# A state-space convolution, an LSTM-like recurrence and a head on one core: GpSimd makes the weights' quarter differences, TensorE transposes the first unit, each tile's two parts go in one DMA transpose, and units and loads come in another order

## The chip, the cores and the metric

The kernel runs on one core of a Trainium2 chip. Its engines work side by side and are tied by semaphores: TensorE (PE: matmuls, and PEld: its weight loads), VectorE (DVE), ScalarE (ACT), GpSimd (POOL) and SyncE (SP), which here issues every DMA; its row is SPq. The metric is the device time in microseconds (us) from the kernel's start to its end, lower is better. The kernel before took 2893.31 us (median of 3 runs, 2892.33 to 2895.29).

## The reference, cut to what matters

```python
x = L0_attn_r                                   # (8, 2048, 512) float32
# 1. state-space layer: K from (B, C, P, Q, Lam, step), a causal convolution over the 2048 rows
h1 = irfft(rfft(norm(x), n=4096) * rfft(K, n=4096))[:, :2048]
x = x + layernorm(gelu(h1 + D * norm(x)))
# 2. a recurrence over the first axis b = 0..7, with 2048 rows x 512 channels as batch
for xt in x:
    ft = sigmoid(xt @ wf.T + c @ uf.T + bf)
    it = sigmoid(xt @ wi.T + c @ ui.T + bi)
    gt = tanh(xt @ wc.T + c @ uc.T + bc)
    c  = ft * c + it * gt                       # c starts as in_c in every row
h = tanh(x @ wo.T + c_final @ uo.T + bo)
x = x + layernorm(h)
```

## The kernel before

**Stages.** From 0 to about 140 us x's statistics and the convolution kernel are made. From there to 640 us the convolution runs in 16 iterations (`i` = 1 to 16), one for each group of 32 channels, each of 16 places `j`. From 640 to 2503 us the recurrence runs, and from there to the end the head (the matmul with wo, tanh, norm, store), 128 tiles of 128 rows.

**Convolution.** In place `j` of iteration `i` PE advances the state of group i (L1700, L1708), applies a power of the state matrix (L1724) and convolves two channels of group i-1 (L1738, L1746). ACT and DVE copy every state and every product of powers out of PSUM as a float16 high part (ACT L923, L934) and a low part (DVE L1276, L1286), and PE's next step waits for them. GpSimd meanwhile normalizes the 4 pieces of group i+1, two operations of 128x1024 a piece (L806 subtracts, L808 multiplies). Beside this the weights are prepared: `weight_places()` puts each step of each of 16 weight loads at an `(i, j)`. Load n is matrix wf, uf, wi, ui, wc, uc, wo or uo; for n % 4 < 2 its largest value is sought (`most`), otherwise it is cut. The six gate matrices are cut into seven "quarters" of 256x256 (a scheme with 7 products for a 2 by 2 block matmul): W11, W21, W22, W12 of the matrix, and three of the four differences made by the step `sum`, which DVE does at L1379, 128x512 each, 4 for each matrix, in iterations 2, 3, 6, 7, 10 and 11 at places 7 to 10. ACT makes each quarter's high part (`hi`, L1009), DVE its low part (`lo`, L1395). `start` is DVE's sum of uf, ui or uc weighted with in_c (L1384, L1386), which stands in for `c @ u.T` where b = 0; it is stored in accd.

**Recurrence.** A unit is 512 rows of one b: b from 0 to 7, and j from 0 to 3 for which quarter of the 2048 rows. There are 32 units, in the order of `unit(u)`: first j = 0 and 1 in turn over all b, then j = 2 and 3. So units 0, 1, 16 and 17 have b = 0 and no product with the state: 42 matmuls a gate group in place of 84. Each unit has 6 gate groups (192 in all); at group n PE makes the products, ACT copies (L1109, L1118, L1125) and applies sigmoid or tanh (L1095), DVE adds (L1557, L1565) and updates the state. Before its products a unit must be prepared in six stages, `prepare(stage, v)` on every engine: load the convolution's result from yd (`load_y`) and x (`load_x1`); DVE's statistics (L1411, L1412), GpSimd's `rate`, ACT's norm (L1017), DVE's `add` of x with statistics (L1419 to L1421), a store of the sum (`store_x1`), a second norm, DVE's `row_sums` (L1436 to L1439, after the store has landed, since they overwrite the tile), the cut in a high part (ACT L1036) and a low part (DVE L1448), and SP's `turn`, which transposes the two parts of each of 8 tiles with a DMA transpose each (L588), 16 a unit. `PREP_AT` says at which gate group each stage of each unit stands: unit 1 at groups 0 to 5, unit 2 at 6 to 11, unit 3 at 12 to 17; units 4, 5 and 6 have only 5 groups each, and from unit 7 on a unit's stages start 9 groups ahead of its own first group. Unit 0's six stages come between convolution and recurrence. Each engine works through its own list in order, and SP's list is one DMA queue, so that order of issue is order of service.

## Time and profile before

| | us |
|---|---|
| median of 3 runs | 2893.31 |
| the profiled execution's own time | 2893.05 |
| its span | 2891.3 |
| PE busy | 2603.2 (90%) |
| PE weight loads | 2105.0 (73%) |
| DVE busy | 1944.9 (67%) |
| ACT busy | 1504.9 (52%) |
| POOL busy | 901.2 (31%) |
| granted TensorE clock, mean | 0.956 of full speed |

"Busy" is time in which the engine executes; an engine that waits is idle. PE is the longest, so what the kernel can lose is mostly time in which PE waits, or runs at the lower clock after it has waited. The rows below come from this one execution.

### The profile page before, as it was taken

Reading aid. Unit: us, or ns where it says so; the run is one execution under the profiler, and the core shown is the slowest. Engines: PE = TensorE matmul, PEld = TensorE weight load, DVE = VectorE, ACT = ScalarE, POOL = GpSimd, SP = SyncE. Lnnn points to the kernel's source line nnn. Section 1 sums busy time; section 2 is a strip of 40 time slices with the busy share of each in tenths; the row PEclk is TensorE's granted clock in tenths of the full one; section 3 lists DMA queues with packets and bytes.
Section 4 is the critical chain, followed back from the end, with each engine's and each line's share of the span. In section 5 each row is a group of like instructions: output and inputs, shape, how many; then the busy total and the mean of one; then the engine's idle time right before and its main releaser. Section 6 shows DMA issues by size and latency. Waiting matters only on the chain.

```text
span 2891.3 us, 55063 instructions
## 1 busy us (share of the span) xinstructions
PE 2603.2 (90%) x21475; PEld 2105.0 (73%) x21475; DVE 1944.9 (67%) x3424; ACT 1504.9 (52%) x2802; POOL 901.2 (31%) x1425
## 2 busy tenths in 40 slices
PE   4598998983679889999999779999999999999997
PEld 4377777873467778888888668888888888744443
DVE  7766667553656666777667577667677775477777
ACT  6655555553544554555555465555455554344444
POOL 7766565521112211211221221221121120043333
PEclk9699999996899999999999989999999999999999
DMA  9877776786444445444534544545644554187776
GB/s 330 289 231 256 244 266 233 266 308 207 112 116 113 99 107 124 121 99 117 130 99 108 155 124 119 128 100 102 124 122 100 121 128 110 62 300 267 268 264 236
DMA packets 541188, 492.06 MB, mean 170 GB/s; under 512 B 292224, under 2 KB 423552, under 8 KB 535680
## 3 DMA queue, kind: packets, MB, share of 16 engines
q1 hardware_dynamic: 540928, 488.56, 57.7%
q8 instruction: 168, 2.75, 0.4%
q14 instruction: 92, 0.75, 0.1%
HBM read 270.60 MB, written 150.73 MB: 146 GB/s over the span
## 4 chain that ended last, share of the span: by engine, by line
PE 53%; DVE 13%; SPq 10%; DMA 9%; ACT 8%; issue 5%; POOL 2%; DVEq 0%; POOLq 0%; ACTq 0%
PE bank L1834 16%; PE bank L1844 15%; SPq L588 9%; PE bank L1902 9%; DMA big<-yd 6%; PE bank L1738 3%; PE bank L1688 3%; ACT big L1095 2%; PE bank L1746 2%; PE bank L1724 2%; DVE big L1539 2%; PE bank L1886 1%; DVE big L1542 1%; DVE big L1379 1%; PE bank L1700 1%
## 5 line engine op out<-in xcount | busy, mean ns | idle before, releaser
L1834 PE MATMUL bank<-big 128*128 128x256 f16 x8064 | 1103.4, 277 | 154.2 <-DMA big<-big 46.7
L1834 PEld LDWEIGHTS bank<-big 128*128 128x128 f16 x8064 | 796.9, 99 | 273.2 <-ACT big L1109 44.1
L1844 PE MATMUL bank<-big 128*128 128x256 f16 x7056 | 967.6, 274 | 0.0
L1844 PEld LDWEIGHTS bank<-big 128*128 128x128 f16 x7056 | 692.9, 98 | 82.2
L851 POOL TENSOR_SCALAR big<-big 128x1 f32<-128x1 f32 x256 | 57.1, 223 | 1397.8 <-DVE big L1412 961.9
L1017 ACT ACTIVATE big<-big 128x512 f32<-128x512 f32 x256 | 206.5, 808 | 272.6 <-POOL big L853 272.1
L1902 PE MATMUL bank<-big 128*128 128x512 f16 x1536 | 332.2, 379 | 0.0
L1095 ACT ACTIVATE big<-big 128x512 f32<-128x512 f32 x384 | 290.9, 805 | 42.4 <-DVE big L1565 42.0
L1902 PEld LDWEIGHTS bank<-big 128*128 128x128 f16 x1536 | 150.3, 98 | 181.2
L1565 DVE TENSOR_TENSOR big<-bank,big 128x512 f32<-128x512 f32 x192 | 130.5, 680 | 182.5 <-PE bank L1844 171.5
L1125 ACT ACTIVATE big<-bank 128x512 f32<-128x512 f32 x192 | 113.3, 590 | 201.0 <-PE bank L1844 191.2
L1411 DVE BATCH_NORM_STATS2 big<-big 128x6 f32<-128x512 f32 x128 | 88.6, 692 | 190.5 <-DMA big<-yd 188.2
L852 POOL TENSOR_TENSOR big<-big 128x1 f32<-128x1 f32 x256 | 200.7, 784 | 21.4
L1118 ACT ACTIVATE big<-bank 128x256 f32<-128x256 f32 x192 | 72.2, 376 | 258.0 <-PE bank L1844 184.6
L806 POOL TENSOR_TENSOR big<-big 128x1024 f32<-128x1024 f32 x63 | 154.6, 2454 | 166.3 <-DMA big<-xg 166.2
L1286 DVE SCALAR_TENSOR_TENSOR big<-bank,big 128x320 f16<-128x320 f32 (+6 forms) x237 | 108.6, 458 | 143.5 <-ACT big L934 143.2
L1135 ACT ACTIVATE big<-big 128x512 f32<-128x512 f32 x128 | 80.7, 630 | 203.8 <-DVE big L1579 203.8
L1448 DVE TENSOR_TENSOR big<-big 128x512 f16<-128x512 f32 x256 | 165.6, 685 | 30.3 <-ACT big L1036 30.1
L1557 DVE TENSOR_TENSOR big<-bank,big 128x512 f32<-128x512 f32 x192 | 131.7, 686 | 76.4 <-ACT big L1109 76.4
L1036 ACT ACTIVATE big<-big 128x512 f16<-128x512 f32 x256 | 153.4, 620 | 48.4 <-DMA big<-big 22.8
L1688 PE MATMUL bank<-big 128*128 128x256 f32 x480 | 152.0, 400 | 15.1 <-DVE big L1268 9.4
L1738 PE MATMUL bank<-big 128*128 128x128 f32 x1024 | 160.8, 280 | 2.1 <-POOL big L817 2.1
(202 smaller groups left out, 3611.5 us busy)
## 6 DMA issues: line engine op xcount, KB each, us to landing
big<-xr SPq DMA_DIRECT2D x16, 2048.0 KB, 10.8
big<-xg SPq DMA_DIRECT2D x64, 512.0 KB, 6.5
big<-kpad SPq DMA_DIRECT2D x32, 1024.0 KB, 12.1
yd<-big SPq DMA_DIRECT2D x16, 2048.0 KB, 17.2
big<-x SPq DMA_DIRECT2D x128, 256.0 KB, 3.1
x1d<-big SPq DMA_DIRECT2D x128, 256.0 KB, 2.0
xtd<-big SPq DMA_DIRECT2D x64, 512.0 KB, 4.6
big<-xtd SPq DMA_DIRECT2D x64, 512.0 KB, 3.9
```

Of the source, the lines that this page charges most:

```text
L588: e.dma_start_transpose(slot[v % 2][:, k, l, :, 128 * p:128 * p + 128], xs16[k][:, l, :]).then_inc(s[f"xq{k}"], 16)
L806: e.tensor_tensor(ug, ug, st(0), SUB).then_inc(s["sub"], 1)
L852: rp().tensor_tensor(st[:, 7:8], st[:, 7:8], mhalf, ALU.pow).then_inc(s["rp"], 1)
L1017: return e.activation(yt[:, :, c, :], e_in, ACT.Identity, bias=st[:, 6:7], scale=st[:, 7:8])
L1036: e.activation(xs16[k][:, 0, :].rearrange("p (g h) -> p g h", g=NG), source(i), ACT.Copy).then_inc(s["xh"], 1)
L1095: e.activation(zt[g][:, r::2, :], zt[g][:, r::2, :], ACT.Tanh if g == 2 else ACT.Sigmoid, bias=bs[:, g, a + 2 * r:a + 2 * r + 1], scale=in ...
L1448: e.tensor_tensor(lo, source(i), hi, SUB).then_inc(s["xlo"], 1)
L1688: ins = e.matmul(o, Gm, u[g % 3][:, k].rearrange("p h b -> p (h b)"), start=True, stop=(k == 0))
L1738: e.matmul(o, T[t % 3][:, h % 16, :], u[g % 3][:, :, h, :], start=(q == 0), stop=False, skip_group_check=True)
L1834: ins = e.matmul(o, WX[2 * g + lw][:, q, kt, 128 * a:128 * a + 128], slot[u % 2][:, part, lx, k0 + kt, :], start=(first and kt == 0 and (l ...
L1844: ins = e.matmul(o, WC[2 * g + lw][:, q, kt, 128 * a:128 * a + 128], cc[u % 2][:, qc, lx, kt, :], start=False, stop=end, skip_group_check= ...
L1902: ins = e.matmul(bank[n % NB_][:, :], xt4[r % NXR][:, lx, kt, 128 * c:128 * c + 128], Wo[:, lw, kt, :], start=(a == 0), stop=(a == 11))
```

## The change

- **Differences.** DVE's step `sum` is gone; GpSimd makes the four differences of a matrix in one go (`quarter_sums`), between the norm of one piece and the next: after the second piece of its iteration, in iteration 2 after the third. The `hi` steps start at place 8 (9 in iteration 2), the `lo` steps one place after each, at 9 to 15 (iteration 2: 10 to 15 and the first of iteration 3).
- **`start` of uf** is done from load 1, at places 0 to 3 of iteration 2, and no longer from load 3; loads 2 and 3 are issued later for it.
- **Unit 0** is no longer prepared in six stages. DVE takes the statistics of the first 15 groups of channels before the last group is done; the second norm writes to other tiles (x0, xs0), so that nothing waits for the store of x1; PE transposes the 8 tiles in float32 into PSUM, and ACT and DVE take the high and low parts from there into the matmuls' operand.
- **SP's order** around this: the load of accd, the last weight stores and loads, and unit 1's loads of x and y ahead of the loads of the state weights (WC).
- **Transposes.** `turn` issues one DMA transpose of 128x1024 for both parts, 8 a unit instead of 16.
- **Order of units**: (7,0), (0,2), (7,1), (0,3) stand at 14 to 17, so that the units with b = 0 of the second half stand at 15 and 17. `last_unit(u)` replaces u - 2 in the waits.
- **`PREP_AT`**: units 1 to 4 take 5 groups each, 1 to 5, 6 to 10, 11 to 15, 16 to 20; then 6 each, 9 groups ahead.
- **Head**: DVE's last addition of a tile comes one tile later (`h - 3` for `h - 2`).

```diff
@@ weight_places
         elif n == 1:
+            places += [("start", f, 2, f) for f in range(4)]
         else:
-            at[n, -1].append(("load", n, 0))
+            at[n, {2: 3, 3: 0}.get(n, -1)].append(("load", n, 0))
...
-                places = [("sum", r, n, 7 + r) for r in range(4)]
-                places += [("hi", q, n, 7 + q) for q in range(7)]
-                places += [("lo", q, n, (9, 11, 12, 13, 14, 15, 15)[q]) for q in range(7)]
+                first = 9 if n == 2 else 8
+                places = [("hi", q, n, min(first + q + (q > 2 and n > 2), 15)) for q in range(7)]
+                places += [("lo", q, n + (first + 1 + q) // 16, (first + 1 + q) % 16) for q in range(7)]
@@ units
+ORDER = [(b, j) for b in range(7) for j in (0, 1)] + [(7, 0), (0, 2), (7, 1), (0, 3)] + [(b, j) for b in range(1, 8) for j in (2, 3)]
 def unit(u):
-    return u % 16 // 2, 2 * (u // 16) + u % 2
+    return ORDER[u]
@@ prep_schedule
-        if v <= 3:
-            places = [6 * (v - 1) + r for r in range(6)]
-        elif v <= 6:
-            first = 18 + 5 * (v - 4)
-            places = [first, first + 1, first + 2, first + 3, first + 4, first + 4]
+        if v <= 4:
+            places = ((1, 2, 3, 4, 5, 5), (6, 7, 8, 9, 10, 10), (11, 12, 13, 14, 15, 15), (16, 17, 18, 19, 20, 20))[v - 1]
@@ SP: turn
-                for l in range(2):
-                    e.dma_start_transpose(slot[v % 2][:, k, l, :, 128 * p:128 * p + 128], xs16[k][:, l, :]).then_inc(s[f"xq{k}"], 16)
+                e.dma_start_transpose(slot[v % 2][:, k].rearrange("p l k t -> p (l k) t")[:, :, 128 * p:128 * p + 128],
+                                      xs16[k].rearrange("p l h -> p (l h)")).then_inc(s[f"xq{k}"], 16)
@@ SP, between convolution and recurrence
+            w.wait_ge(s["accs"], 16 * 3)
+            e.dma_start(fbs, accd.rearrange("g p h -> p g h")).then_inc(s["accs"], 16)
             load_WX(4)
             load_WX(5)
...
+            store_y(NG - 2)
             store_y(NG - 1)
+            w.wait_ge(s["cv"], G * NG)
+            for r in range(4):
+                store_x1(0, r)
+            for c in CHUNKS:
+                load_x1(1, c)
+            load_y(1)
...
+            for n in range(6):
+                load_WC(n)
+            store_xt(0)
@@ GpSimd
+            def quarter_sums(n):
+                m = 2 * (n // 4) + n % 2
+                w.wait_ge(s["w"], 16 * (n + 1))
+                w.wait_ge(s["w_hi"], low_base(m))
+                w.wait_ge(s["w_lo"], low_base(m))
+                for o, p0, p1 in ((Wt[0], W12, W11), (Wt[1], W22, Wt[0]), (W12, W22, W12), (Wt[2], W21, Wt[1])):
+                    ws().tensor_tensor(o, p0, p1, SUB).then_inc(s["w_sum"], 1)
+            for i in range(1, NG - 1):
+                for q in range(4):
+                    norm(4 * (i + 1) + q)
+                    if i < 12 and i % 4 >= 2 and q == (2 if i == 2 else 1):
+                        quarter_sums(i)
@@ PE, ahead of unit 0 (ACT's high and DVE's low read bank[2 + i % 6])
+            for i in range(8):
...
+                for kt in range(4):
+                    ins = e.transpose(bank[2 + i % 6][:, kt * 128:(kt + 1) * 128], source(i)[:, kt * 128:(kt + 1) * 128], ident)
@@ DVE, ahead of unit 0
+            for n in range(4):
+                stat(n)
+            w.wait_ge(s["fb"], 12)
+            e.tensor_tensor(bias0, bank[0][:, 0:12].rearrange("p (g m) -> p g m", g=3), bias, ADD).then_inc(s["yc"], 1)
+            for n in range(4):
+                add(n)
+            row_sums(0, 0)
+            low(0)
+            row_sums(0, 1)
+            for i in range(1, 8):
+                low(i)
```

The order on VectorE in iteration 6, places 7 to 11, before (L1379 is `sum`, L1395 `lo`, L1276 and L1286 the parts that PE's next step waits for):

```order
362 L1379 TENSOR_TENSOR big<-big 128x512
363 L1276 SCALAR_TENSOR_TENSOR big<-bank,big 128x256
364 L1286 SCALAR_TENSOR_TENSOR big<-bank,big 128x8x32
365 L1379 TENSOR_TENSOR big<-big 128x512
366 L1276 SCALAR_TENSOR_TENSOR big<-bank,big 128x256
367 L1286 SCALAR_TENSOR_TENSOR big<-bank,big 128x6x64
368 L1379 TENSOR_TENSOR big<-big 128x2x256
369 L1395 SCALAR_TENSOR_TENSOR big<-big 128x512
```

and after, from place 9 on (L1432 is `lo`, L1323 and L1333 are L1276 and L1286):

```order
360 L1432 SCALAR_TENSOR_TENSOR big<-big 128x512
361 L1323 SCALAR_TENSOR_TENSOR big<-bank,big 128x256
362 L1333 SCALAR_TENSOR_TENSOR big<-bank,big 128x6x64
363 L1432 SCALAR_TENSOR_TENSOR big<-big 128x512
364 L1323 SCALAR_TENSOR_TENSOR big<-bank,big 128x256
365 L1333 SCALAR_TENSOR_TENSOR big<-bank,big 128x5x64
366 L1432 SCALAR_TENSOR_TENSOR big<-big 128x512
```

The four differences are gone from DVE's list, and the low parts stand one at a place from 9 on. On GpSimd the four stand in iteration 6 after the second of four pieces (L824 and L826 are L806 and L808, L869 the differences):

```order
184 L824 TENSOR_TENSOR big<-big 128x1024
185 L826 TENSOR_TENSOR big<-big 128x1024
186 L824 TENSOR_TENSOR big<-big 128x1024
187 L826 TENSOR_TENSOR big<-big 128x1024
188 L869 TENSOR_TENSOR big<-big 128x512 x2
189 L869 TENSOR_TENSOR big<-big 128x2x256
190 L869 TENSOR_TENSOR big<-big 128x512
191 L824 TENSOR_TENSOR big<-big 128x1024
192 L826 TENSOR_TENSOR big<-big 128x1024
```

The norm of the third and fourth piece now comes behind them. SP's list from the end of the convolution to unit 1's first transposes, before:

```order
114 L557 DMA big<-yd 128x14x128
115 L572 DMA big<-x 128x512 x4
116 L470 DMA yd<-big 128x4096
117 L475 DMA big<-wg 128x3584 x2
118 L630 DMA big<-accd 128x3x512
119 L480 DMA big<-wg 128x3584 x3
120 L470 DMA yd<-big 128x4096
121 L480 DMA big<-wg 128x3584 x3
122 L577 DMA x1d<-big 128x512 x4
123 L588 DMA_TRANSPOSE big<-big 128x4x128 x12
124 L572 DMA big<-x 128x512 x2
125 L564 DMA big<-yd 128x16x128
```

and after:

```order
114 L568 DMA big<-yd 128x14x128
115 L587 DMA big<-x 128x512 x4
116 L643 DMA big<-accd 128x3x512
117 L486 DMA big<-wg 128x3584 x2
118 L481 DMA yd<-big 128x4096 x2
119 L592 DMA x1d<-big 128x512 x4
120 L587 DMA big<-x 128x512 x4
121 L576 DMA big<-yd 128x16x128
122 L491 DMA big<-wg 128x3584 x6
123 L609 DMA xtd<-big 128x2048 x2
124 L592 DMA x1d<-big 128x512 x4
125 L602 DMA_TRANSPOSE big<-big 128x8x128 x6
```

The load of accd moved ahead of two weight loads and a store, unit 0's transposes are gone, and unit 1's x and y stand ahead of the six state weight loads.

## Rows read from the trace of the kernel before

**Rows 1.** Iterations 3, 5, 6, 7; length; busy of PE, PEld, DVE, ACT, POOL; clock; DMA
```profile
204.80:246.90 42.10, 33.85 (x282) 27.62 (x279) 30.77 (x47) 20.81 (x45) 20.63 (x8) 0.88 0.65 225
276.80:306.50 29.70, 29.61 (x285) 25.11 (x282) 17.18 (x41) 16.66 (x38) 19.05 (x8) 1.00 0.73 248
306.50:342.60 36.10, 30.98 (x280) 25.73 (x278) 24.55 (x44) 20.70 (x45) 20.11 (x8) 0.95 0.63 212
342.60:378.80 36.20, 29.96 (x282) 24.66 (x279) 27.14 (x43) 20.59 (x45) 20.56 (x8) 1.00 0.74 255
```

**Rows 2.** Waits of PE from 190 to 640 us: for whom, us, times, longest
```profile
PE bank L1708 <- DVE big L1276: 33.9, 27, 4.1
```

**Rows 3.** Groups by line, 190 to 640 us: busy us, mean ns, idle before
```profile
L1379 DVE TENSOR_TENSOR big<-big 128x512 f32<-128x512 f32 x24 | 44.0, 1834 | 0.0
L1395 DVE SCALAR_TENSOR_TENSOR big<-big 128x512 f16<-128x512 f32 x42 | 40.8, 995 | 0.0
```

**Rows 4.** Timeline of iteration 6, DVE and POOL: start, us, engine, line
```profile
329.52 2.70 POOL L808 TENSOR_TENSOR big<-big 128x1024 f32<-128x1024 f32 x1
329.91 2.86 DVE L1395 SCALAR_TENSOR_TENSOR big<-big 128x512 f16<-128x512 f32 x1
333.49 0.67 DVE L1379 TENSOR_TENSOR big<-big 128x512 f32<-128x512 f32 x1
```

**Rows 5.** Timeline of PE from the convolution's end: start, us, [idle before <-releaser]
```profile
652.99 5.25 PE L1820 MATMUL bank<-big 128*128 128x1 f32 x24 [12.68 <-DMA big<-accd]
690.00 1.44 PE L1834 MATMUL bank<-big 128*128 128x256 f16 x6 [31.76 <-issue]
700.86 4.45 PE L1834 MATMUL bank<-big 128*128 128x256 f16 x20 [9.42 <-DMA big<-big]
```

**Rows 6.** Timeline of SP's queue, 640 to 700 us
```profile
648.41 27.05 SPq L577 DMA_DIRECT2D x1d<-big  x4
675.56 15.75 SPq L588 DMA_TRANSPOSE big<-big  x12
...
692.53 0.38 SPq L564 DMA_DIRECT2D big<-yd  x1
```

**Rows 7.** Line 630, the load of accd issued at 637.4 us: issue to landing
```profile
DMA to landing us min/median/max: 15.4/15.4/15.4
```

**Rows 8.** Timeline of DVE, preparation of unit 0, and unit 1's first statistics
```profile
645.21 0.69 DVE L1419 TENSOR_TENSOR big<-big 128x512 f32<-128x512 f32 x1
...
646.98 0.69 DVE L1419 TENSOR_TENSOR big<-big 128x512 f32<-128x512 f32 x1
...
672.70 0.42 DVE L1436 TENSOR_TENSOR big<-big 128x256 f32<-128x256 f32 x1 [12.39 <-DMA x1d<-big]
...
699.84 0.69 DVE L1411 BATCH_NORM_STATS2 big<-big 128x6 f32<-128x512 f32 x1 [11.19 <-DMA big<-yd]
```

**Rows 9.** Stretches: unit 0, unit 1, units 2 to 5, unit 6, unit 16
```profile
700.90:747.70 46.80, 30.88 (x247) 25.11 (x248) 28.59 (x54) 24.77 (x44) 10.71 (x25) 0.83 0.54 135
747.70:805.20 57.50, 35.71 (x258) 27.42 (x258) 38.43 (x67) 29.73 (x52) 10.67 (x25) 0.80 0.44 110
805.20:1064.70 259.50, 231.41 (x2020) 201.67 (x2021) 166.50 (x276) 126.32 (x217) 56.31 (x117) 0.94 0.43 108
1064.70:1120.00 55.30, 54.36 (x499) 48.48 (x498) 38.66 (x63) 30.01 (x52) 11.49 (x24) 1.00 0.49 115
1622.50:1676.50 54.00, 36.40 (x292) 30.04 (x290) 36.30 (x64) 31.25 (x55) 10.92 (x25) 0.84 0.53 140
```

**Rows 10.** Waits of PE from 805 to 1065 us
```profile
PE bank L1834 <- ACT big L1109: 13.4, 4, 7.2
```

**Rows 11.** Line 588, the transposes, 1060 to 1560 us: ns min/median/max, and landing
```profile
L588 SPq DMA_TRANSPOSE big<-big x144: 1188/1266/5400, 1070.9 to 1543.3; - x144
...
DMA to landing us min/median/max: 2.4/2.5/8.5
```

**Rows 12.** The chain that ended last, in the head: start, us, what
```profile
2700.40 82.88 PE bank L1902 x384
```

More of the change, by code:

```diff
@@ L311, in s4_lstm_program @@
         junk = take(1)
+        st0 = [take(12) for _ in range(4)]
         winv = win.rearrange("p (k o) -> p k o", k=4)
@@ L841, in pool_program @@
             norm(7)
-            for n in range(8, 4 * NG):
-                norm(n)
+            ws = Chain(w, s, "w_sum")
+            def quarter_sums(n):
[10 more added lines that the diff above has]
+                        quarter_sums(i)
             rp = Chain(w, s, "rp")
@@ L866, in prepare @@
                     rate(4 * v + 3, "2")
-            for stage in range(1, 7):
-                prepare(stage, 0)
+            for n in range(4):
+                rate(n, "1")
+            for n in range(4):
+                rate(n, "2")
             for n in range(GROUPS):
@@ L1069, in state_high @@
             def state_high(u, place):
-                c16, last = cc[u % 2], unit(u)[0] == 7
+                b, j = unit(u)
+                c16, c32, last = cc[j % 2], cf[j % 2], b == 7
                 if place == 0:
@@ L1491, in state_sums @@
             def state_sums(u, place):
-                c32, last = cf[u % 2], unit(u)[0] == 7
+                c32, last = cf[unit(u)[1] % 2], unit(u)[0] == 7
                 base = state_parts(u - 1) if u else 0
```

171 lines of the change are left out of this document (99 added, 72 removed).

## The prediction

> **What bounds the kernel now.** I read the page's busy shares and slices first: PE is busy 90% of the span, so what can be saved is where PE waits or runs at the lower clock. The busy times by stretch show three such places. In the convolution most iterations last 29.7 us with PE busy in nearly all of it, while iterations 6 and 7, with the same number of matmuls, last 36.1 and 36.2 us, and iteration 3 lasts 42.1 [rows 1]. Iterations 10 and 11 look like 6 and 7 (35.6 and 36.9 us between the same points). PE's waits there are on DVE's low part of the state, 33.9 us in 27 waits [rows 2]. The second place is 640 to 701 us, where PE does almost nothing [rows 5]. The third is the recurrence's units that PE does not fill: a settled unit lasts 55.3 us with PE busy 54.4, but unit 0, with half the matmuls, lasts 46.8, unit 1 57.5 and unit 16 54.0, and units 2 to 5 last 259.5 where four settled ones would be 221 [rows 9]. In the head the chain of waits is PE without a gap [rows 12]. Everything else is PE at 2.4 GHz and isn't touched.
>
> **The convolution.** The edit takes 24 differences, 44.0 us in all, off DVE [rows 3]. Their time alone isn't the cost. One such difference takes 0.67 us when GpSimd is idle; a low part that starts 0.39 us after a GpSimd multiply takes 2.86 us, ending 0.55 after it [rows 4]. So the two engines exclude one another when both read SBUF with two operands, and DVE loses up to 2.1 us beyond its 0.74. Of 42 low parts only the excess of (0.995 - 0.74) x 42 = 10.7 us is there, five or six long ones: the low parts of an iteration now come mostly after GpSimd has ended its norm. That cover goes. GpSimd has 8 operations of 2.4 us (busy 19 to 20 us of an iteration) [rows 1], and four differences of half the elements, 1.2 us each, come between them: 25 of 29.7 us. It will then be busy at places 9 to 15, where the low parts now stand. By places (1.8 us each), GpSimd starting about 5 us into iteration 6 as now (its last multiply ends at 332.2 [rows 4], 25.7 in, of which 20.1 busy): two pieces to 15, differences to 20, two pieces to 30. The low parts at places 9, 10, 11 (16 to 20 us) meet short operations, those at 12 and 13 (21 to 25) long ones; those at 14 and 15 have no close follower, since no state is advanced at 15. A long meeting makes a place 2.9 us instead of 1.8, so 1.1 each; a short one I take at 0.2. That is 2.8 us, near 3 with the clock, against 36.1 - 29.7 = 6.4 today. Iterations 6, 7, 10, 11: 4 x 3.7 = 15. Iteration 3 has `start` and the differences today, 42.1 - 29.7 = 12.4; left with 4, it gives 8. Iteration 2 gets `start` at places 0 to 3 and later loads: it loses 1. Sum -22. Bounds: the excess of all six iterations is 45 (no meeting costs anything); if each of five low parts an iteration costs the full 2.1, 6 x 10.5 = 63 is left instead of 45: 18 slower.
>
> The Trainium skill ("SBUF — State Buffer", section "SBUF: two separate sides") says that VectorE and GpSimd share a port pair as an exclusive lock held for the whole instruction, for a VectorE operation with two SBUF inputs among others. It speaks against the edit: the lock time isn't removed but moved to the other side of it. The 2.86 us agree. By the rule alone, with the low parts always met, the second bound would be nearer.
>
> **Convolution to recurrence.** Today: convolution ends at 640.3, the load of accd lands 15.4 us after its issue [rows 7], the bias matmuls run 653.0 to 658.2 [rows 5], unit 0's row sums wait 12.4 us for the store of x1 [rows 8], which lies behind six weight loads and two stores, then the transposes take 675.6 to 691.3 with a row of their own each [rows 6], and PE's products run steadily from 700.9 [rows 5]. After: accd lies only behind y and x, so about 645.5 by the same queue; bias matmuls 5.2, to 650.7. DVE now waits for them before its four `add`s, 1.77 us each [rows 8], to 657.9. Row sums 1.8 (659.7), rate, second norm and first high part (660.7), its low part, row sums of the other half 663.2, PE's transposes of the last two tiles about 3 (at the rate of the 24 small float32 matmuls in 5.25 us [rows 5], 1.8 for a tile's four), their high and low parts 1.3: PE starts near 669. That is 32 us. Nothing else is late: the weights of the inputs land before, the state weights (six loads of 0.9 MB) are first needed by unit 2, 100 us later.
>
> Unit 1's y can be issued when six tiles are cut, 667, and lands 7.3 later, 674.5 (today 692.5 to 699.8 [rows 6, 8]). Its preparation took 699.8 to 747.7, 48 us, by the chain DVE, GpSimd, ACT, SP, not by PE [rows 9]; I take 47 in five groups. Unit 1 starts at 721.5 instead of 747.7: -26 up to here. Its own length stays 57.5: PE's 12 short groups of units 0 and 1 are fewer than preparation needs. Unit 2 starts with its transposes already landed, but in unit 1's last group DVE waits for unit 3's y.
>
> Units 2 to 5 hold 38 us beyond four settled ones [rows 9]. Partly these are waits for transposes and partly the wait for y, 11.2 us for DVE in the first case [rows 8], which reaches PE through ACT L1109 (13.4 us, up to 7.2) [rows 10] and costs clock on top. It is exposed where stages 5 and 6 of one unit and stage 1 of the next stand in adjacent groups, today at three places in units 3 to 5, and the transposes come last at two more. After, two such places are left (groups 16 and 21), about 10 us each: 38 becomes 21, -17. Sum of this part: -43. Bounds: if the 5-group schedule costs as much as today, -26; if the excess vanishes and units 0 and 1 follow at PE's pace, -75.
>
> **One transpose for two.** A transpose now takes 1.27 us of SP's queue, in a chain of 2.5 to landing [rows 11]; 16 are 20 us of a 55 us unit. The larger one isn't in the trace: between 1.27 us (a cost per instruction) and twice or more. Twelve took 15.75, 1.31 each, with hardly a gap [rows 6], and each moves 128 KB; I take the double, 2.5, so nothing gained. The Trainium skill ("DMA: Bandwidth & Descriptors", section "Why a DMA increments its semaphore by 16 and not by 1") gives for the sequencers before the newest chip a push command per tile of a transpose, so a cost in proportion to size; the sum would be the same.
>
> **Order of units.** Unit 16 is 26 us longer than PE's half unit; 10 of it is DVE's wait for y. That wait stays, in units 15 and 17 now, since stage 1 still falls in the middle of every unit. What a long unit between them gives is one group of slack once more: -3, between +5 and -15. **Head**: PE is the bound without gaps [rows 12], so DVE's later addition is worth 0; if it made DVE late, the last tile's addition of about 0.7 us is all that the end could see.
>
> **The sum.** -22 - 43 - 3 = -68 on the profiled execution's 2893.05 (span 2891.3; median of the runs 2893.31, the same within 0.3): 2825 us.
>
> **Rivals.**
> A. *The lock eats the convolution's gain.* All exposed low parts meet long operations: no gain or a loss of up to 18 there. For it: GpSimd is made busier exactly where low parts stand. Against it: the differences are short, and five places an iteration are exposed, not seven. With 0 there: 2847.
> B. *The merged transpose costs as one.* For it: it is one instruction, and the queue's 1.27 us hardly vary; against it, the size. SP's 12 transposes ahead of the y load shrink by 8 us; where y and the last transposes are exposed (units 0 to 3, 15, 17), 3 to 4 us each: -20. 2805.
> C. *The recurrence starts no earlier than its data*: stores of y and x1, unit 1's x and y and the state weights share one queue, and unit 1's x1 store lands behind 5.4 MB of weights. Today's wait of that kind was 12.4 us [rows 8]. With 15 us lost: 2840.
> D. *Slower: the merged transpose is worse than two.* Place: SP's queue. A unit there has 8 merged transposes and about 6 us of other issues; PE's unit is 55. From about 6 us each the queue is as long as the unit. Each further us costs 8 us in 28 long units, 224; the gain of 68 is gone at 6.3 us, and at 7 us the time is about 3050. Nothing in the trace shows such a cost, only that the shape is new.
>
> **Chances.** Forecast 0.45 (2800 to 2850), A 0.2, B 0.18, C 0.12, D 0.05. The range 2790 to 2862 holds the forecast, A, B and C, each with some 15 us of its own uncertainty cut off at the edge. A measurement of this kernel can tell 0.2%, 6 us, from no change: faster 0.94, same 0.01, slower 0.05.
>
> **What would show it.** In iterations 6, 7, 10, 11: length near 33 us, no differences on DVE, low parts of 1.3 to 2.9 us at places 12 and 13. At 2.86 everywhere, or lengths over 36, A holds. PE's products start near 669 less what the convolution gave (about 647 on the new clock of events), unit 1 some 52 us later. The transposes' row: 2.5 us is the forecast, 1.3 is B, over 6 is D. Units 2 to 5 near 242 us. Units 15 and 17 with PE idle some 18 us each; if it is under 8, slack was worth more than I gave it. The forecast is wrong if the recurrence's settled units differ from 55.3 us, which nothing here should touch.

## The result, and the profile after

The kernel after took 2778.23 us (median of 4 runs, 2775.45 to 2780.31), the kernel before 2893.85 on the same chip (4 runs, 2892.33 to 2895.29): ratio 0.96, 95% interval 0.9583 to 0.9617. It is 115.6 us faster; 68 were forecast, and 2778 lies below the range. The profiled executions differ by as much: span 2891.3 before, and from the page of the kernel after (its first line, and PE's busy time):

```profile
span 2777.9 us, 54870 instructions
...
PE 2591.0 (93%) x21507; PEld 2101.9 (76%) x21507; DVE 1941.2 (70%) x3404; ACT 1511.5 (54%) x2802; POOL 959.8 (35%) x1449
```

Cut at the same instructions in both traces, the 113.4 us of the spans lie here (us; "forecast" is the prediction's own term for the stretch; the convolution is taken from PE's first to its last matmul of L1738, L1799 after, "steady products" begin at 700.9 before and 644.9 after):

| stretch | before | after | change | forecast |
|---|---|---|---|---|
| to the convolution's first matmul | 138.7 | 137.5 | -1.2 | 0 |
| convolution, 16 iterations | 501.1 | 481.8 | -19.3 | -22 |
| its end to the steady products | 61.1 | 25.7 | -35.4 | -32 |
| recurrence (to the head's first matmul with wo) | 1812.9 | 1760.8 | -52.1 | -14 |
| head | 377.5 | 372.1 | -5.4 | 0 |

**Convolution.** Stretches of the kernel after, iterations 3, 6, 7 (length, busy of PE, PEld, DVE, ACT, POOL, clock, DMA), against [rows 1]:

```profile
204.60:237.30 32.70, 29.55 (x280) 24.68 (x278) 21.27 (x37) 20.44 (x46) 23.17 (x11) 1.00 0.84 294
...
298.20:329.70 31.50, 29.45 (x281) 24.76 (x280) 21.01 (x38) 19.71 (x44) 25.58 (x12) 1.00 0.74 256
329.70:362.30 32.60, 29.95 (x280) 24.81 (x278) 22.24 (x38) 20.54 (x46) 23.02 (x12) 1.00 0.81 282
```

Iterations 6, 7, 10 and 11 together went from 144.9 to 128.8, iteration 3 from 42.1 to 32.7, iteration 2 from 34.1 to 35.2. But 4, 8 and 12, which were 29.9, 29.3 and 29.3, are 31.3, 31.1 and 31.1. These are single executions: in the profiles of the experiments below that leave the convolution as it is, it takes 497.6 to 501.0 us in the kernel before and 481.1 to 484.8 in the kernel after (iteration 3 alone 39.5 to 41.8 and 32.7 to 37.0), so the gain is known to some 4 us. GpSimd is busy 25.6 of 31.5 us in iteration 6, and DVE's low parts meet it. Groups by line, 190 to 620 us of the kernel after, for [rows 3]:

```profile
L1432 DVE SCALAR_TENSOR_TENSOR big<-big 128x512 f16<-128x512 f32 x42 | 65.4, 1568 | 0.0
...
L869 POOL TENSOR_TENSOR big<-big 128x512 f32<-128x512 f32 x24 | 32.6, 1357 | 3.3 <-DMA big<-wts 1.9
```

A low part now takes 1.57 us in the mean instead of 0.995. The timeline of DVE's low parts in iteration 6:

```profile
318.12 0.96 DVE L1432 SCALAR_TENSOR_TENSOR big<-big 128x512 f16<-128x512 f32 x1
...
320.04 1.85 DVE L1432 SCALAR_TENSOR_TENSOR big<-big 128x512 f16<-128x512 f32 x1
...
322.54 2.13 DVE L1432 SCALAR_TENSOR_TENSOR big<-big 128x512 f16<-128x512 f32 x1
...
325.33 2.14 DVE L1432 SCALAR_TENSOR_TENSOR big<-big 128x512 f16<-128x512 f32 x1
...
330.93 0.73 DVE L1432 SCALAR_TENSOR_TENSOR big<-big 128x512 f16<-128x512 f32 x1
```

and of GpSimd there, the differences and the norm of the pieces behind them:

```profile
313.22 5.31 POOL L869 TENSOR_TENSOR big<-big 128x512 f32<-128x512 f32 x4
318.49 2.85 POOL L824 TENSOR_TENSOR big<-big 128x1024 f32<-128x1024 f32 x1
321.42 2.71 POOL L826 TENSOR_TENSOR big<-big 128x1024 f32<-128x1024 f32 x1
324.08 2.83 POOL L824 TENSOR_TENSOR big<-big 128x1024 f32<-128x1024 f32 x1
326.99 2.72 POOL L826 TENSOR_TENSOR big<-big 128x1024 f32<-128x1024 f32 x1
```

While GpSimd works on 128x1024, each low part waits and ends 0.55 us after the GpSimd operation that it met (at 321.34, 324.13 and 326.91), which by then has been followed by the next; the one at 330.93, past GpSimd's last multiply (329.7), takes 0.73. Each of these meetings costs the low part 1.1 to 1.4 us. The full 2.0 to 2.1 us of [rows 4] is still there once in each of iterations 3, 7 and 11, where a low part of 2.78 us starts just behind a GpSimd operation. In each of iterations 6, 7, 10 and 11 four low parts last 1.85 us or more. PE's waits on DVE's low part of the state, 190 to 620 us, for [rows 2]:

```profile
PE bank L1769 <- DVE big L1323: 18.4, 21, 1.7
```

33.9 us became 18.4, and the longest wait 1.7 instead of 4.1.

**Convolution to recurrence.** Timeline of PE in the kernel after, for [rows 5] (start, us, and in brackets the idle time before it and its releaser):

```profile
623.27 4.72 PE L1881 MATMUL bank<-big 128*128 128x1 f32 x24 [3.45 <-DMA big<-accd]
632.29 1.11 PE L1892 MATMUL bank<-big 128*128 128x128 f32 x4 [4.30 <-ACT big L1050]
...
641.41 0.63 PE L1892 MATMUL bank<-big 128*128 128x128 f32 x4 [0.50 <-DVE big L1498]
644.95 2.29 PE L1909 MATMUL bank<-big 128*128 128x256 f16 x10 [2.91 <-issue]
```

The wait for accd is 3.45 us instead of 12.68, PE's own transposes (L1892) take 632.3 to 642.0, and products run from 644.95.

**Recurrence.** Stretches of the kernel after: unit 0, unit 1, units 2 to 5, unit 6, for [rows 9]:

```profile
644.70:693.60 48.90, 31.55 (x252) 24.62 (x252) 29.53 (x55) 25.06 (x44) 9.38 (x24) 0.88 0.80 250
693.60:747.00 53.40, 36.82 (x261) 28.16 (x262) 37.82 (x67) 27.83 (x49) 11.00 (x26) 0.82 0.51 123
747.00:982.00 235.00, 224.74 (x1998) 197.89 (x1997) 165.85 (x274) 127.61 (x218) 54.55 (x116) 0.97 0.49 118
982.00:1037.00 55.00, 55.00 (x506) 49.29 (x505) 39.53 (x64) 30.35 (x52) 11.75 (x24) 1.00 0.48 116
```

Units 2 to 5 take 235.0 (259.5 before), and a settled unit has PE busy in all of its 55.00 us. The transposes, 980 to 1430 us, for [rows 11]:

```profile
L602 SPq DMA_TRANSPOSE big<-big x64: 1232/1290/3390, 990.5 to 1396.9; - x64
...
DMA to landing us min/median/max: 3.1/3.4/6.6
```

One transpose of 128x1024 takes 1.29 us of the queue, where one of 128x512 took 1.27. It costs as one, not as two. What that does is seen in SP's queue. One settled unit of the kernel before, from the stores of x1 (L577) over 12 transposes (L588) and two loads of x (L572) to the load of the next unit's y (L564):

```profile
1108.40 18.45 SPq L577 DMA_DIRECT2D x1d<-big  x4
1127.02 18.11 SPq L588 DMA_TRANSPOSE big<-big  x12
1145.17 1.06 SPq L572 DMA_DIRECT2D big<-x  x2
1146.27 0.43 SPq L564 DMA_DIRECT2D big<-yd  x1
```

and of the kernel after (L592, L602, L587, L576):

```profile
1024.23 21.09 SPq L592 DMA_DIRECT2D x1d<-big  x4
1045.49 13.31 SPq L602 DMA_TRANSPOSE big<-big  x6
1058.86 1.05 SPq L587 DMA_DIRECT2D big<-x  x2
1062.03 0.38 SPq L576 DMA_DIRECT2D big<-yd  x1
```

Before, the y load follows the x loads without a gap, 19.2 us after the first transpose, and in the last 12 us before it the queue is never idle: the queue sets when it goes. After, it goes 16.5 us after it, and 2.1 us of that SP waits for DVE's row sums, which free y's tile: now the data set it. DVE's waits for y in the whole execution of the kernel before (us in total, times, longest):

```profile
DVE big L1411 <- DMA big<-yd: 188.2, 31, 11.2
```

and of the kernel after:

```profile
DVE big L1455 <- DMA big<-yd: 79.9, 30, 8.6
```

How such a wait reaches PE, in a settled unit of the kernel before: DVE's first statistics of the next unit,

```profile
1153.98 0.69 DVE L1411 BATCH_NORM_STATS2 big<-big 128x6 f32<-128x512 f32 x1 [5.39 <-DMA big<-yd]
```

and PE 9 us on:

```profile
1162.90 0.83 PE L1834 MATMUL bank<-big 128*128 128x256 f16 x6 [1.04 <-ACT big L1118]
```

DVE stands still for 5.39 us with the gates' additions behind it. ACT's sigmoid (L1095) waits for such an addition, DVE's next additions for the sigmoid, ACT's copy (L1118) for these, and PE for the copy: it loses 1.04. From 980 to 1100 us of the kernel after DVE's wait is 1.5 to 1.7 us, and PE has none.

### The profile page after: what moved, and what is told of

Read it like the earlier page. It is cut to its first block, busy times and chain, and to the rows that moved or that the text cites. A ratio compares the mean times of both kernels' runs of the same rounds, so it can differ in the third digit from the quotient of the medians.

```text
span 2777.9 us, 54870 instructions
## 1 busy us (share of the span) xinstructions
PE 2591.0 (93%) x21507; PEld 2101.9 (76%) x21507; DVE 1941.2 (70%) x3404; ACT 1511.5 (54%) x2802; POOL 959.8 (35%) x1449
## 4 chain that ended last, share of the span: by engine, by line
PE 80%; DVE 8%; DMA 4%; ACT 3%; issue 2%; POOL 1%; SPq 1%; DVEq 0%; POOLq 0%; ACTq 0%
PE bank L1909 28%; PE bank L1919 27%; PE bank L1977 12%; PE bank L1749 3%; PE bank L1799 3%; PE bank L1785 2%; PE bank L1807 2%; DVE big L1432 2%; PE bank L1961 1%; DMA big<-yd 1%; PE bank L1761 1%; DMA big<-big 1%; DMA big<-xr 1%; DVE big L1344 1%; PE bank L1769 1%
## 5 line engine op out<-in xcount | busy, mean ns | idle before, releaser
L1333 DVE SCALAR_TENSOR_TENSOR big<-bank,big 128x320 f16<-128x320 f32 (+6 forms) x237 | 108.5, 458 | 140.4 <-ACT big L968 140.1
L824 POOL TENSOR_TENSOR big<-big 128x1024 f32<-128x1024 f32 x63 | 154.1, 2446 | 111.6 <-DMA big<-xg 111.4
L1504 DVE TENSOR_TENSOR big<-big 128x512 f16<-128x512 f32 x248 | 159.8, 684 | 6.7 <-ACT big L1077 6.6
L1799 PE MATMUL bank<-big 128*128 128x128 f32 x1024 | 159.1, 278 | 2.1 <-POOL big L835 2.1
L826 POOL TENSOR_TENSOR big<-big 128x1024 f32<-128x1024 f32 x63 | 154.8, 2457 | 4.9
## 6 DMA issues: line engine op xcount, KB each, us to landing
big<-xr SPq DMA_DIRECT2D x16, 2048.0 KB, 11.1
```

The lines of the kernel that those rows point to most:

```text
L824: e.tensor_tensor(ug, ug, st(0), SUB).then_inc(s["sub"], 1)
L826: e.tensor_tensor(ug, ug, st(1), MUL).then_inc(s["nrm"], 1)
L1504: e.tensor_tensor(lo, source(i), hi, SUB).then_inc(s["xlo"], 1)
L1799: e.matmul(o, T[t % 3][:, h % 16, :], u[g % 3][:, :, h, :], start=(q == 0), stop=False, skip_group_check=True)
```

## The experiments

The kernel before took 2893.9 to 2900.7 us on the chips used; differences under some 6 us between kernels of different chips are therefore read from stretches of the profile, not from medians. "Marks" of units are ACT's copies (L1109 before, L1156 after), one a gate group; the first six units lie between the first mark and the 37th. Stretches scatter too: five other profiles of the kernel after whose edits lie outside the first six units (experiments 6 and 8 to 10) or change the transposes' number alone (13) have 336 to 337 us there, where the kernel after's own has 340.7.

**1. The merged transpose alone** (kernel before, with it).

```diff
-                for l in range(2):
-                    e.dma_start_transpose(slot[v % 2][:, k, l, :, 128 * p:128 * p + 128], xs16[k][:, l, :])...
+                e.dma_start_transpose(slot[v % 2][:, k].rearrange("p l k t -> p (l k) t")[:, :, 128 * p:128 * p + 128], xs16[k].rearrange("p l h -> p (l h)"))...
...
```

> The kernel before with one DMA transpose for both parts of a tile, nothing else changed. Theory 1 (the larger transpose costs SP's queue as much as one small one, 1.29 us, so that the y load comes earlier in every unit and the small stalls of the settled units go): 25 to 45 us faster than before, the settled units at 55.0 us each as in the changed kernel. Theory 2 (the forecast's: cost in proportion to size, the shorter settled units come from another part of the change): within 5 us of before, and settled units of 55.2 to 56 us.

2818.51 us (2816.33 to 2819.36), before on that chip 2897.17: ratio 0.9734 [0.972, 0.9749], 79 us faster by one edit that was priced at nothing, and far more than theory 1's 25 to 45. DVE's waits for y:

```profile
DVE big L1411 <- DMA big<-yd: 82.8, 31, 8.0
```

**2. All but the merged transpose** (kernel after, with two again: edit 1 backwards).

> The changed kernel with two DMA transposes a tile again. Theory 1: it gives back 25 to 45 us, to 2803 to 2823. Theory 2: within 5 us of 2778. If it gives back clearly less than the same edit brings to the kernel before, the other parts of the change have hidden part of the cost.

2837.54 us (2832.77 to 2841.55): ratio 0.98 [0.9782, 0.9818], 58 us slower than experiment 6 (the kernel after with the old order of units) on the same chip; again more than the 25 to 45 expected. All other parts together bring 56 to 60, where the sum had 68. The same edit brings the kernel before 79, so the other parts hide some 20 of it. DVE's waits for y are back:

```profile
DVE big L1455 <- DMA big<-yd: 177.9, 30, 9.7
```

**3. The y load earlier, two transposes** (kernel of experiment 2, in SP's list of a unit).

```diff
                 if stage == 5:
-                    for k in range(2, 6):
-                        turn(8 * v + k)
-                    if v + 1 < NU:
-                        load_x1(v + 1, 0)
-                        load_x1(v + 1, 2)
+                    turn(8 * v + 2)
+                    turn(8 * v + 3)
                 if stage == 6:
                     if v + 1 < NU:
                         load_y(v + 1)
+                    turn(8 * v + 4)
+                    turn(8 * v + 5)
+                    if v + 1 < NU:
+                        load_x1(v + 1, 0)
+                        load_x1(v + 1, 2)
```

> The kernel after with two transposes a tile again (2837.5 us by itself, 59 more than with one), and with the y load ahead of the transposes of tiles 4 and 5 and of the loads of x. Theory (two transposes cost 59 us because some 5 us more of queue stand ahead of the y load in each unit): with four transposes fewer ahead of it a good part of the 59 comes back, 2785 to 2810, and the waits for y, 177.9 us in 30 waits without the move, fall below 110. Rival (what two transposes cost is their own landing and the products that wait for tiles): it stays at 2830 or more.

2776.36 us (2773.12 to 2777.1): ratio 0.9576 [0.9556, 0.9596]. All 61 us are back, more than the theory gave, though its 16 transposes a unit fill the queue as before. DVE's waits for y are 52.5 us. The queue in a settled unit, with 8 transposes ahead of y in place of 12:

```profile
1043.59 12.75 SPq L603 DMA_TRANSPOSE big<-big  x8
1060.11 0.38 SPq L576 DMA_DIRECT2D big<-yd  x1
```

It goes 16.5 us after the first transpose, as in the kernel after. So the 61 us come back by a shorter queue ahead of the y load, with the transposes' own number and landing as they were. That the merged transpose gains nothing by its own landing doesn't follow: see experiment 5.

**4. The same in the kernel before** (that edit alone).

> The kernel before with one edit: the load of the next unit's y ahead of the transposes of tiles 4 and 5 and of the two loads of x in SP's list of a unit; still two transposes a tile. Theory (what the merged transpose brought is queue time ahead of the y load, and any edit that lets this load start earlier brings the same): as in the kernel before with merged transposes, 2800 to 2830, and the waits for y, 188 us in 31 waits, fall below 100. Rival (in the kernel before something else holds the units, the early load brings only what the kernel after leaves on it, 14 us): 2870 to 2885.

2837.91 us (2834.48 to 2841.91): ratio 0.9792 [0.977, 0.9813], 62 us faster, 8 outside the theory's interval and far from the rival's. The waits for y fall to 55.3 us. Merging brings 17 to 19 us more than this in the kernel before, though the early y load leaves DVE less to wait: 10.0 of them by the recurrence's first mark (3.4 of these in the convolution, which neither edit touches, the others where unit 0 is transposed), 11.7 in units 0 to 5. The sum of the waits is thus a sign and not a price.

**5. The y load earlier in the kernel after** (edit of experiment 3).

> The kernel after, with the load of the next unit's y put into SP's list of a unit ahead of the transposes of tiles 4 and 5 and of the two loads of x, instead of behind them. Theory (what the merged transpose gave back is time that stood ahead of the y load in that queue, and the rest of the wait for y, 79.9 us in 30 waits in the kernel after, is more of the same): the waits for y fall by half or more, the time falls by 20 to 40 us, to 2740 to 2760. Rival (the wait for y in the kernel after is set by when the exchange of y is written, not by the queue; the merged transpose gained by its own landing): within 5 us of the kernel after, 2773 to 2783; if tiles 4 and 5 then come late to the products, up to 10 us slower.

2764.56 us (2763.65 to 2772.0): ratio 0.954 [0.9519, 0.9561]. 14 us faster than the kernel after: between theory and rival. The waits fall only to

```profile
DVE big L1457 <- DMA big<-yd: 59.1, 30, 3.3
```

because SP now waits for the row sums: 56.1 us in 8 units of 980 to 1430 us (22.9 in the kernel after):

```profile
SPq L576 <- DVE big L1493: 56.1, 8, 7.1
```

The gain lies in units 0 to 5 (327.9 us by marks, 340.7 after) and 15 and 17; settled units have nothing left to give. Against experiment 3, which differs from this one in the merging alone and ran on the same chip (2776.36), it is 11.8 us faster, 11.0 of them in units 0 to 5: there the merged transpose still brings something when y is early. Whether that is the transposes' landing or the rest of the queue was not tried apart.

The recurrence of seven kernels, us between marks:

| kernel | units 0-5 | 6-17 | 18-30 | DVE's waits for y |
|---|---|---|---|---|
| before | 364.8 | 656.9 | 727.1 | 188.2 |
| before, merged (1) | 330.1 | 641.3 | 715.3 | 82.8 |
| before, y early (4) | 341.8 | 639.2 | 715.3 | 55.3 |
| after, split (2) | 363.2 | 660.1 | 726.4 | 177.9 |
| after, split, y early (3) | 338.9 | 636.1 | 715.8 | 52.5 |
| after | 340.7 | 641.3 | 715.3 | 79.9 |
| after, y early (5) | 327.9 | 635.8 | 715.3 | 59.1 |

715.3 is 13 units of 55.0, PE's own time. Every kernel here that gets y early, by either edit, reaches it within 0.5; with the rest of the change alone it is 726.4.

**6. The old order of units** (kernel after).

```diff
-ORDER = [(b, j) for b in range(7) for j in (0, 1)] + [(7, 0), (0, 2), (7, 1), (0, 3)] + [(b, j) for b in range(1, 8) for j in (2, 3)]
+ORDER = [(b, j) for b in range(8) for j in (0, 1)] + [(b, j) for b in range(8) for j in (2, 3)]
```

> The changed kernel with the old order of units (all of j = 0 and 1, then j = 2 and 3), so that both short units of the second half stand next to each other at 16 and 17; the preparation's schedule as in the changed kernel. Theory 1 (each short unit pays DVE's wait for y and the preparation's chain by itself, wherever it stands): 0 to 4 us slower than the changed kernel. Theory 2 (a long unit between the short ones gives back slack, and that is the 10 us found in units 14 to 17 beyond the 3 forecast): 7 to 12 us slower.

2779.22 us (2777.11 to 2781.08): ratio 0.9599 [0.9585, 0.9614]. No difference. Units 14 to 17 take 201.2 us by marks, with the new order 201.1.

**7. The old places of preparation** (kernel after, `PREP_AT` of units 1 to 6 as before).

> The changed kernel with the old places of units 1 to 6 in the preparation's schedule (unit 1 at groups 0 to 5, 6 groups each up to unit 3, 5 groups each for units 4 to 6). Theory 1 (as in the forecast: the new places take one exposed wait for y and the late transposes of units 2 to 4 away): 12 to 20 us slower than the changed kernel. Rival (with the cheaper transpose and the earlier y the places hardly matter): under 5 us slower.

2773.86 us (2772.61 to 2780.37): ratio 0.9568 [0.9551, 0.9584]. If anything faster: from the first products to the head's first matmul 1753.2 us against 1760.8, and against 1756.4 to 1757.3 in experiments 6, 8, 9, 10 and 13. Once the merged transpose is there, the five-group places bring nothing. What they bring with two transposes was not tried.

**8. The differences on DVE** (kernel after; `sum`, the places of `hi` and `lo`, `start` and the loads as before).

```diff
+                places = [("sum", r, n, 7 + r) for r in range(4)]
+                places += [("hi", q, n, 7 + q) for q in range(7)]
+                places += [("lo", q, n, (9, 11, 12, 13, 14, 15, 15)[q]) for q in range(7)]
...
-                    if i < 12 and i % 4 >= 2 and q == (2 if i == 2 else 1):
-                        quarter_sums(i)
```

> The changed kernel with the quarter differences back on DVE, at the old places, and loads and start steps as before. Theory 1 (as in the forecast): it gives back what the convolution brought, 19 us between the same points of the two traces, so 17 to 21 us slower than the changed kernel, iterations 6 and 7 at 36 us. Rival (the convolution's shorter time comes from other loads and is not the differences): under 8 us.

2794.09 us (2791.8 to 2796.81): ratio 0.9633 [0.9619, 0.9648], 16 slower than the kernel after. Theory 1 holds, a little short of its 17 to 21. The convolution takes 499.0 us against 481.8, iterations 3, 6, 7, 10, 11: 39.6, 34.6, 36.8, 36.7, 37.3.

**9. GpSimd nearly idle where low parts stand** (kernel after; in iterations 6, 7, 10 and 11 the norm of pieces 3 and 4 is done on 8 elements a row instead of 1024, so most of it is left out).

```diff
...
+                if g in (7, 8, 11, 12) and q >= 2:
+                    ug, st0_, st1_ = ug[:, 0:1, 0:1], st0_[:, 0:1, 0:1], st1_[:, 0:1, 0:1]
...
```

> The changed kernel in which GpSimd leaves out most of the norm of the third and fourth piece of the input in iterations 6, 7, 10 and 11 (the two operations act on 8 elements a row instead of 1024), so that GpSimd is idle while DVE makes its low parts. Theory 1 (DVE's low parts wait for GpSimd's operations, which exclude them from SBUF): low parts of 0.74 us there, iterations 6, 7, 10, 11 at 29.5 to 30 instead of 31.5 to 32.7 us, 7 to 11 us faster in all. Rival (they last longer because of ACT's high parts or of DVE's own list): no change within 2 us.

2763.29 us (2762.31 to 2764.65): ratio 0.9527 [0.9513, 0.9541], and 14.5 less than experiment 13 (2777.81, no different from the kernel after) on the same chip, where 7 to 11 were expected. Its iterations 6 and 7:

```profile
300.90:330.00 29.10, 29.03 (x281) 24.69 (x279) 17.14 (x40) 19.67 (x44) 15.75 (x12) 1.00 0.82 280
330.00:359.90 29.90, 29.38 (x281) 24.76 (x279) 18.00 (x38) 20.37 (x46) 16.44 (x12) 1.00 0.88 309
```

All four are PE's own 29.1 to 29.9 us (10.5 less together, as expected), and so are 8 and 12 (29.6, where the kernel after has 31.1; another 3.0): the excess there was GpSimd's work that had slid into them. With GpSimd quiet the low parts take 0.73 to 0.75 us each and cost PE nothing. PE's waits, 190 to 620 us:

```profile
PE bank L1772 <- DVE big L1326: 6.8, 9, 1.7
```

**10. The norm in halves** (kernel after; pieces 3 and 4 in iterations 2, 3, 6, 7, 10, 11, each operation as two of 128x512).

```diff
+                cuts = ((0, 2), (2, 4)) if g in (3, 4, 7, 8, 11, 12) and q >= 2 else ((0, 4),)
...
+                    for a, b_ in cuts:
+                        ins = e.tensor_tensor(ug[:, a:b_], ug[:, a:b_], st(r)[:, a:b_], op)
```

> The kernel after with GpSimd's normalisation of pieces 3 and 4 in iterations 2, 3, 6, 7, 10 and 11 in operations of half the size (128x512 elements instead of 128x1024), the same work in all. Theory (DVE's low parts are held up only while a whole GpSimd operation holds the port, so shorter operations let DVE in between): 3 to 10 us faster than the kernel after, 2768 to 2775. Rival (the port's total time counts, not the length of a hold): within 2 us, or up to 5 us slower by the fixed time of twelve times four more operations.

2769.67 us (2767.35 to 2772.45): ratio 0.9552 [0.9535, 0.957]; the convolution takes 475.8 us, 6.0 less, with the same work. Low parts in its iteration 6:

```profile
319.30 0.83 DVE L1436 SCALAR_TENSOR_TENSOR big<-big 128x512 f16<-128x512 f32 x1
...
321.33 1.86 DVE L1436 SCALAR_TENSOR_TENSOR big<-big 128x512 f16<-128x512 f32 x1
...
323.85 1.04 DVE L1436 SCALAR_TENSOR_TENSOR big<-big 128x512 f16<-128x512 f32 x1
```

and PE's waits, 190 to 620 us:

```profile
PE bank L1773 <- DVE big L1327: 10.1, 12, 1.4
```

The gain is within the theory's 3 to 10. The length of one GpSimd operation counts, not GpSimd's total.

**11. accd late** (kernel after; the load of accd behind a store of y and two weight loads again).

```diff
-            w.wait_ge(s["accs"], 16 * 3)
-            e.dma_start(fbs, accd.rearrange("g p h -> p g h")).then_inc(s["accs"], 16)
+            store_y(NG - 2)
             load_WX(4)
             load_WX(5)
-            store_y(NG - 2)
+            w.wait_ge(s["accs"], 16 * 3)
+            e.dma_start(fbs, accd.rearrange("g p h -> p g h")).then_inc(s["accs"], 16)
```

> The kernel after with the order of SP's list behind the convolution put back in one point: the load of the accumulated columns (accd), which the bias products wait for, stands behind the store of y and the two loads of weights 4 and 5 again. If the earlier start of the recurrence comes from TensorE's own transposes alone: as the kernel after, 2776 to 2782. If it needs the early load too: the stretch from the end of the convolution to the products grows from 25 us by 5 to 10, and the time to 2782 to 2790.

2786.54 us (2785.11 to 2789.19): ratio 0.9616 [0.96, 0.9632]. PE waits for it again:

```profile
634.90 5.25 PE L1881 MATMUL bank<-big 128*128 128x1 f32 x24 [12.90 <-DMA big<-accd]
```

The end of the convolution to the first products is 35.7 us, 10.0 more. So 10 of the 35.4 us won there belong to this load, the other 25 to TensorE's transposes with the order of the other stores and loads and the tiles that spare the wait for x1's store, which were not tried apart.

**12. The head's later addition** (kernel before, `head_out(h - 3)` in place of `h - 2`).

> The kernel before with DVE's last addition of a head tile one tile later, nothing else. Theory 1 (in the head DVE's chain with ACT, 2.75 us a tile, is slower than PE's 2.59, so the end hangs on it): 4 to 6 us faster, tail behind PE's last matmul some 9 us instead of 15. Theory 2 (the forecast's: PE bounds the head, the edit is worth 0): within 2 us of before.

2889.06 us (10 runs, 2883.93 to 2895.36): ratio 0.9972 [0.996, 0.9985], 8 us less than the kernel before on that chip (4 to 12 by the interval), and the head 372.1 us, 5.4 less, as in the kernel after. Groups of DVE from 2520 to 2860 us in the kernel before (busy, mean ns, idle before and releaser):

```profile
L1579 DVE SCALAR_TENSOR_TENSOR big<-bank,big 128x512 f32<-128x512 f32 x118 | 87.9, 745 | 6.4 <-PE bank L1902 6.4
L1592 DVE TENSOR_TENSOR big<-big 128x512 f32<-128x512 f32 x117 | 81.0, 692 | 68.4 <-ACT big L1140 68.4
```

and 2412 to 2752 us in the kernel after:

```profile
L1653 DVE TENSOR_TENSOR big<-big 128x512 f32<-128x512 f32 x117 | 81.1, 693 | 15.9 <-DVE big L1648 0.5
```

Before, DVE waited 0.58 us in each tile for ACT and hardly for PE: it was a chain of its own, 2.75 us a tile (its L1579 at 2796.27, 2799.03, 2801.78) against PE's 2.59 (82.88 us for 32 tiles, [rows 12]), and fell behind. The banks hid this until PE was done: from PE's last matmul to the end were 14.7 us before, 9.3 after.

**13. One transpose for two tiles** (kernel after; 128x2048, 4 a unit).

```diff
+                if k % 2 == 0:
+                    return
+                e.dma_start_transpose(slot[v % 2][:, k - 1:k + 1].rearrange("p q l k t -> p (q l k) t")[:, :, 128 * p:128 * p + 128],
+                                      f16(x0_at + 512 * (k - 1), 1024)).then_inc(s[f"xq{k - 1}"], 16)
...
```

> The changed kernel with one DMA transpose for two tiles and both their parts (128x2048), 4 a unit instead of 8. Theory 1 (the queue's cost is one of an instruction, some 1.3 us whatever its size up to here): queue time of 1.3 to 1.5 us each, and 0 to 8 us faster, since the preparation is exposed only in units 0 to 3, 15 and 17. Theory 2 (the cost grows with size beyond 128x1024): 2.6 us or more each, and no gain, or a loss of up to 5 us because a transpose now waits for two tiles.

2777.81 us (2776.76 to 2780.99): ratio 0.958 [0.9564, 0.9597], no difference that can be told from the kernel after. Its transposes, 980 to 1430 us:

```profile
L605 SPq DMA_TRANSPOSE big<-big x33: 1317/2289/4442, 988.9 to 1429.0; - x33
...
DMA to landing us min/median/max: 4.3/5.0/7.3
```

From here on the queue's time does grow with the size, by 1.8 for the double: neither theory's number.

**14 and 15. Versions that put the two remaining causes together**: halves (10), early y (5) and old places (7); and halves with early y alone.

> The kernel after with three edits together: the halves of GpSimd's normalisation, the early y load, and the places of the transposes of units 1 to 6 as in the kernel before. If the gains of the three (expected -5, -25, and -4 as measured) add up: about 2745. If the y load's rival holds: about 2768.

2763.5 us (2759.55 to 2768.57): ratio 0.9532 [0.9511, 0.9553], so the three don't add up. Without the old places:

> The kernel after with the halves of GpSimd's normalisation (8 us by itself) and the early y load (14 us by itself), without the third edit of the version with three. If the two add up: 2756 to 2760. If the units that the early load frees hide what the halves bring: 2762 to 2765, as the version with three.

2755.3 us (2751.49 to 2759.08): ratio 0.9507 [0.9488, 0.9526]. The two add up (convolution 476.0 us, units 0 to 5 328.0). From the convolution's end over unit 5 it takes 361.1 us, and 365.2 with the old places (359.3 in experiment 5): beside an early y the old places seem to cost some 4 to 6 us, which is near the scatter. The version with two edits beats both kernels, the kernel after by about 23 us.

## Why the prediction was wrong

- **The step that failed is the price of the merged transpose**, "I take the double, 2.5, so nothing gained". It takes 1.29 us, not 2.5. The evidence given for the double was that twelve transposes took 1.31 each with hardly a gap; that shows what one costs and says nothing of size. The bound at 1.27 was written down, and the choice between ends far apart went to the wrong one. The Trainium skill ("DMA: Bandwidth & Descriptors", section "Why a DMA increments its semaphore by 16 and not by 1") has one push command per tile before the newest chip, which the prediction read as a cost in proportion to size. From 128x512 to 128x1024 the queue's time grew by 2%, and only at 128x2048 to 2.29 us, so up to 128x1024 the measurement goes against that reading.
- **Rival B named the mechanism and under-priced it.** It gave -20 for "units 0 to 3, 15, 17". The runs show 58 us in the kernel after and 79 in the kernel before. By marks, from experiment 2 to the kernel after, the merging brings 22.5 in units 0 to 5, 18.8 in 6 to 17 and 11.1 in 18 to 30, where B counted units 0 to 3, 15 and 17 alone. DVE's waits for y, 188.2 us in 31 times, stood in the waits of the whole execution; the prediction looked at the first one and at two stretches, and took them as exposed only "where stages 5 and 6 of one unit and stage 1 of the next stand in adjacent groups". They stood in every unit, and in the settled ones each cost PE 0.9 us in the mean (units 18 to 30: 727.1 against 715.3).
- **"Everything else is PE at 2.4 GHz and isn't touched"**, and settled units of 55.3 that "nothing here should touch": PE busy 54.4 of 55.3 [rows 9] was read as PE's bound. The 0.9 us left was the wait for y seen from PE, and other units had more (up to 59). After, it is 55.00 of 55.00.
- **From the convolution's end over unit 5** (-43 forecast: the earlier start, the places of preparation, units 2 to 5). With two transposes still, in experiment 2, this stretch fell from 432.0 to 396.2 us, -35.8: the steady products 34.1 earlier (32 forecast; the terms as written end at 667.5 and not near 669, which would be 33), unit 1 by 24 (26), units 2 to 5 by 13.1 (17). The merged transpose takes 24 more from it in the kernel after. That the places of preparation had a part is not shown: put back with merged transposes (experiment 7), the time does not rise. **Order of units**: -3 forecast, nothing measured (experiment 6). PE is idle for 13.4 us in unit 15, between the 18 expected and the 8 that would have told of slack; what units 14 to 17 gain on the kernel before, 211.4 to 201.1 us, comes by the earlier y, under either order.
- **Convolution**: right in kind, -22 forecast and -19.3 measured, iterations 6, 7, 10, 11 by 16.1 (15), iteration 3 by 9.4 (8), iteration 2 +1.1 (+1). Missed are 5.0 us in iterations 4, 8 and 12. That the single iterations fit so well is in part luck: two long meetings an iteration were counted at 1.1 us of PE's time each, and there are four, which cost the low parts 1.1 to 2.0 us each, but the iteration only 1.8 to 3.0 us in all over 29.7. Rival A falls: experiment 8 loses 17 us of the convolution. The two engines do exclude each other, as the Trainium skill says ("SBUF — State Buffer", section "SBUF: two separate sides"): a low part that meets a GpSimd operation ends 0.55 us after it. Experiments 9 and 10 agree, the second by the length of one GpSimd operation alone.
- **Rival C** falls: the recurrence starts 35.4 us sooner after the convolution, 10 of them by the load of accd (experiment 11).
- **Head**: "PE is the bound without gaps", and so a worth of 0, read only PE's chain up to its last matmul. DVE's 68 us of waits for ACT showed that DVE was slower a tile than PE; the end saw 5.4 us of it.
- **Rival D** falls by the 1.29 us.

## What to carry to other kernels

When a queue issues in order, write down for each load what stands ahead of it and whether the queue idles before it; a load that follows its predecessor without a gap is late by all that stands ahead, and moving it can be worth nearly as much as making what stands ahead cheaper (in the kernel before 62 us by a few lines, against 79). Total an engine's waits for one load over the whole execution before pricing them unit by unit, and don't call an engine the bound at 98% busy. A price that lies between two far ends for an operation not in the trace is a coin toss; give the other end its full, worked-out gain.

## What the runs showed of the hardware

- A DMA transpose of float16 from SBUF to SBUF takes 1.27 us of its queue at 128x512, 1.29 at 128x1024 and 2.29 at 128x2048 (medians, 980 to 1430 us of kernels 2, after and 13); it lands 2.5, 3.4 and 5.0 us after its issue.
- GpSimd's float32 operations with two operands: 128x1024 2.39 us alone, 2.7 to 2.85 with DVE's low parts beside them; 128x512 1.27 alone and 1.6 to 1.7 so (kernel after). Both engines lose.
- DVE's low part of 128x512: 0.73 to 0.75 us with GpSimd quiet; in a row of GpSimd's 128x1024 operations 2.13 to 2.15, and 2.78 when it starts just behind the first (kernel after); in a row of 128x512 0.83 to 1.86 (experiment 10).
- TensorE's transposes of a 128x512 float32 tile, four matmuls, take 0.63 to 1.11 us (kernel after, 632 to 642 us, mean granted clock 0.56; the prediction had 1.8).
